# Two pairs of blocks merged, and idle products on TensorE at the end of the sorted experts' layer

## The reference

```python
def _L2_attn_ref(x, Wq, bq, Wk, bk, Wv, bv, Wo, bo):      # 16 heads of 16
    q = einsum('btc,hcd->bhtd', x, Wq) + bq;  k = ... + bk;  v = ... + bv
    probs = softmax(q @ k.T * scale + causal)
    return (probs @ v) @ Wo + bo

def _L2_ffn_ref(x, weight, scale, expert_masks, router_w): # top 1 of 32 experts
    p = softmax(x @ router_w)
    return max(p) * (x @ (ternary(weight) * scale * expert_masks[argmax(p)]).T)

def _L3_attn_ref(x, Wq_a, q_norm_w, Wq_b, Wk_rope, Wkv_a, kv_norm_w, Wkv_b, Wo):
    q = rmsnorm(x @ Wq_a, q_norm_w) @ Wq_b                 # latent of 192
    kv = rmsnorm(x @ Wkv_a, kv_norm_w) @ Wkv_b             # latent of 64
    k_rot = rope(x @ Wk_rope)                              # 64, shared by the heads
    return causal_attention(q, kv, k_rot) @ Wo
```

## Time and profile before

| | |
|---|---|
| median of 3 executions | 1505.15 us (1503.67 to 1508.03) |
| profiled execution, its own time | 1509.29 us |
| its span, first to last instruction | 1506.8 us |
| busy in the span | PE 1308.7, DVE 790.2, ACT 588.9, POOL 416.4 us |
| mean granted TensorE clock | 0.927 of full |

### The profile page before, as it was taken

One profiled execution on the slowest core, in us unless ns is written; L12 is line 12 of the kernel. 1 busy time (PEld: TensorE's weight loads), 2 busy tenths in 40 slices (PEclk: granted clock), 3 DMA queues, 4 the chain that ended last, 5 costly groups with the idle time before them and its releaser, 6 DMA issues. The chain is left out here.

```text
span 1506.8 us, 29274 instructions
## 1 busy us (share of the span) xinstructions
PE 1308.7 (87%) x12212; PEld 1002.6 (67%) x12235; DVE 790.2 (52%) x1491; ACT 588.9 (39%) x1067; POOL 416.4 (28%) x346
## 2 busy tenths in 40 slices
PE   6879989979989979899979889999779578969988
PEld 3468985559957667788747667888755234557555
DVE  5734465553272633433528556888245547943543
ACT  4612224483534653334412521223324333641551
POOL 0063302034730000445320105443011219921100
PEclk9979999989989999999978889999889789989999
DMA  4000003054041001000090060000044210000000
GB/s 107 0 2 4 3 4 113 1 118 96 1 130 60 2 1 32 1 0 1 1 263 31 21 216 1 1 1 2 1 162 154 73 19 1 2 1 29 2 1 28
DMA packets 75266, 63.56 MB, mean 42 GB/s; under 512 B 21240, under 2 KB 73152, under 8 KB 75008
## 3 DMA queue, kind: packets, MB, share of 16 engines
q1 hardware_dynamic: 72320, 58.90, 13.7%
q0 software_dynamic: 768, 2.10, 0.4%
q10 hardware_dynamic: 2048, 0.70, 0.2%
HBM read 53.29 MB, written 8.39 MB: 41 GB/s over the span
## 5 line engine op out<-in xcount | busy, mean ns | idle before, releaser
L1796 PE MATMUL ps<-rounded 128*128 128x512 f32 x384 | 92.9, 398 | 5.9 <-DVE work L1928 5.3
L1482 POOL TENSOR_TENSOR work<-weights,work 32x512 f32<-32x512 f32 x64 | 85.9, 1342 | 17.9 <-DVE work L1469 14.0
L1264 POOL TENSOR_TENSOR fixed<-fixed,cross 128x768 f32<-128x768 f32 x32 | 58.8, 1838 | 110.7 <-DVE cross L1213 110.7
L1796 PEld LDWEIGHTS ps<-rounded 128*128 128x128 f32 x384 | 72.2, 191 | 24.6 <-issue 6.3
L1178 PE MATMUL ps<-rounded 128*128 128x256 f32 x576 | 79.5, 294 | 6.8 <-DVE rounded L1232 4.1
L1827 POOL TENSOR_TENSOR rounded<-weights,rounded 128x256 fp32r<-128x256 f32 x32 | 23.6, 757 | 205.3 <-ACT rounded L1845 205.3
L1178 PEld LDWEIGHTS ps<-rounded 128*128 128x128 f32 x576 | 73.3, 197 | 10.2 <-DVE rounded L1232 4.4
L211 PE MATMUL ps<-fixed 128*128 128x128 f32 x160 | 35.8, 352 | 46.7 <-ACT fixed L199 28.3
L211 PEld LDWEIGHTS ps<-fixed 128*128 128x128 f32 x160 | 20.6, 169 | 60.1 <-issue 33.0
L716 DVE TENSOR_TENSOR fixed<-fixed,ps 128x512 f32<-128x512 f32 x12 | 8.2, 687 | 99.2 <-PE ps L632 99.2
L1928 DVE TENSOR_TENSOR work<-work,ps 128x512 f32<-128x512 f32 x32 | 22.0, 687 | 68.4 <-ACT work L1862 66.3
(11 more groups left out here) (472 smaller groups left out, 3239.8 us busy)
## 6 DMA issues: line engine op xcount, KB each, us to landing
weights<-in_L_ffn_masksT SPq DMA_DIRECT2D x32, 256.0 KB, 6.3
weights<-in_L_ffn_fc_w SPq DMA_DIRECT2D x16, 256.0 KB
weights<-in_L_xattn_Wq SPq DMA_DIRECT2D x2, 2048.0 KB, 9.9
weights<-in_L_xattn_WoT SPq DMA_DIRECT2D x2, 2048.0 KB, 10.2
sorted_in<-work SPq DMA_DIRECT2D x1, 3072.0 KB, 10.6
work<-sorted_in SPq DMA_DIRECT2D x12, 256.0 KB, 3.0
sorted_out<-work SPq DMA_DIRECT2D x12, 256.0 KB, 2.1
weights<-in_L_ffn_Wg SPq DMA_DIRECT2D x8, 256.0 KB, 6.1
```

Source lines behind the costliest of these rows:

```text
L1264: nc.gpsimd.tensor_tensor(ro[:, v % 2, :, :], ro[:, v % 2, :, :], sn, ALU.add).then_inc(s["roped"], 1)
L1482: last = nc.gpsimd.tensor_tensor(qb[64 + 32 * half:96 + 32 * half, 2 * (u % 2) + e, tok], cs[made, v % 2, :], sn[made, v % 2, :], ALU.add)
L1796: last = nc.tensor.matmul(ps[:, 2 * (n % 2) + i, :], a[:, q % 2, i, c, :], b[:, c, half * BANK:(half + 1) * BANK], start=c == 0 and part = ...
```

## The change

It has three parts.

1. **L2_attn**: the two blocks become one. TensorE goes from the keys' products to the values' products, and waits only for the copy of the queries whose banks the values take (`queries`, 1 for the first eight sequences, 2 for the rest). The first scores wait for the copied keys (`keys`) too. POOL clears `vblk` first, then adds the bias to `x`, then clears `blank`. SP's clearing DMA stands behind the same loads as before, now in this block.
2. **L3_attn**: the two blocks ahead of the attention become one. DVE handles the latents in two halves of four tiles, ACT's queue interleaves squares, the two roots and the repeated part, TensorE turns each half behind the latents, and the copies out are shared: ACT takes the first half and one of the two last copies (`values`), DVE the second half and the other. `hold(k, 7, 10)` takes the place of `hold(k, 6, 10)`.
3. **L2_ffn**: `hold(k, 2, 48)` after the last `apply`, and `hold(k, 2, 4)` after the first and after the second `norm_turn`.

```diff
@@ stage_L3_attn, the first two blocks
-    with k.stage("sorted", "lat", "sq", "mean", "std", "rstd", "qn", "km", "kvn", "kra", "krb") as (block, s):
+    lat = qb[0:64, 3, :]
+    with k.stage("sorted", "lat", "sq", "mean", "std", "rstd", "qn", "dup", "kvn", "kra", "krb", "vzero", "t_qn", "t_km", "c_qn", "c_km",
+                 "c_lat", "t_kv", "kvs") as (block, s):
+        def copied(eng, scaled, copy, g):
+            eng.wait_ge(s["t_qn"], g + 1)
+            for a in range(2):
+                ins = scaled(qnT[:, a, g * BANK:(g + 1) * BANK], ps[:, 4 * g + a, :], (w.qw, w.qw_low)[a][:, 1:2])
+            ins.then_inc(s["c_qn"], 1)
+            eng.wait_ge(s["t_km"], g + 1)
+            copy(kk[:, g * BANK:(g + 1) * BANK], ps[:, 4 * g + 2, :]).then_inc(s["c_km"], 1)
+            for jp in range(2):
+                ins = copy(lat[...], ps[0:64, 4 * g + 2, ...])
+            ins.then_inc(s["c_lat"], 1)
+        def values(eng, copy, jj):
+            eng.wait_ge(s["t_kv"], 1)
+            eng.wait_ge(s["vzero"], 1)
+            copy(kvt[rows, :, jj, :], ps[rows, 3, :]...).then_inc(s["kvs"], 1)
@@ TensorE, behind the eight latents
+            for g in range(2):
+                pe.wait_ge(s["krb"], g + 1)
+                pe.wait_ge(s["kvn"], 4 * g + 4)
+                pe.wait_ge(s["dup"], 4 * g + 4)
+                (8 transposes of qn, then_inc t_qn; 4 transposes of km, then_inc t_km)
+            hold(k, 7, 10)
+            pe.wait_ge(s["c_lat"], 2)
+            (8 transposes of lat, then_inc t_kv)
@@ ScalarE
+            for j in range(5):
+                squares(j)
+            root(0)
+            squares(5)
+            again(0)
+            again(1)
+            squares(6)
+            again(2)
+            again(3)
+            squares(7)
+            root(1)
+            copied(act, ..., nc.scalar.copy, 0)
+            for j in range(4, NT):
+                again(j)
+            values(act, nc.scalar.copy, 0)
@@ VectorE: for g in range(2), on tiles 4g to 4g+3
+                dve.wait_ge(s["lat"], 4 * g + 4)
+                dve.wait_ge(s["sq"], 8 * g + 8)
+                (rope products, means, rope sum, reciprocal, scaling, as before on half the tiles)
+            copied(dve, ..., nc.vector.tensor_copy, 1)
+            values(dve, nc.vector.tensor_copy, 1)
@@ stage_L2_ffn, TensorE
                 apply(b)
+            hold(k, 2, 48)
             for i in range(NT // 2):
                 norm_turn(k, s, pe, i, (0, 1))
+                if i < 2:
+                    hold(k, 2, 4)
@@ stage_L2_attn, the two blocks in one
-    with k.stage("bk", "qk", "copied", "xb") as (block, s):
...
-    with k.stage("v", "vzero", "vals", ...) as (block, s):
+    with k.stage("bk", "qk", "queries", "keys", "xb", "v", "vzero", "vals", ...) as (block, s):
             for b in range(BATCH):
+                if b % 8 == 0:
+                    pe.wait_ge(s["queries"], b // 8 + 1)
...
                 if u == 0:
                     pe.wait_ge(s["vals"], 4)
+                    pe.wait_ge(s["keys"], 4)
...
             nc.gpsimd.memset(vblk, 0.0).then_inc(s["vzero"], 1)
+            pool.wait_ge(w.sem, w.loaded)
+            nc.gpsimd.tensor_tensor(x, x, bc(w.bo, 1, NT), ALU.add).then_inc(s["xb"], 1)
             nc.gpsimd.memset(blank, 0.0).then_inc(s["blank"], 1)
...
             normalise(7)
+            dve.wait_ge(s["xb"], 1)
```

More of the change, by code:

```diff
@@ L1350, in _, with squares @@
                         nc.gpsimd.tensor_copy(to[:, :, n, e, :], of[:, :, e, n, :]).then_inc(s["sorted"], 1)
+            nc.gpsimd.memset(kvt, 0.0).then_inc(s["vzero"], 1)
         @block.scalar
         def _(act):
-            for j in range(NT):
+            def squares(j):
                 act.wait_ge(s["lat"], j + 1)
@@ L1360, in _, with root, again @@
                 nc.scalar.activation(sq[:, 0:64], ps[:, j, 192:256], ACT.Square, accum_out=ss[:, 1, j:j + 1]).then_inc(s["sq"], 1)
-            act.wait_ge(s["mean"], 2)
-            nc.scalar.activation(rstd, ss, ACT.Sqrt).then_inc(s["std"], 1)
-            for j in range(NT):
+            def root(g):
+                act.wait_ge(s["mean"], 2 * g + 2)
+                nc.scalar.activation(rstd[:, :, 4 * g:4 * g + 4], ss[:, :, 4 * g:4 * g + 4], ACT.Sqrt).then_inc(s["std"], 1)
+            def again(j):
@@ L1389, in stage_L3_attn @@
[L1389 to L1392, removed]
-            for g in range(2):
[L1394 to L1432, removed]
@@ L2308, in stage_L2_attn, with _ @@
     mx, sm, rs = k.work.take(2, 16), k.work.take(2, 16), k.work.take(2, 16)
-    with k.stage("bk", "qk", "copied", "xb") as (block, s):
+    blank = k.work.take(D)
+    with k.stage("bk", "qk", "queries", "keys", "xb", "v", "vzero", "vals", "scored", "maxed", "centred", "expd", "summed", "recip", "probs", "turned", "copied", "pv",
+                 "yT", "out", "added", "blank", "cleared", *NORM_SEMS) as (block, s):
+        @block.sync
+        def _(sp):
+            sp.wait_ge(s["blank"], 1)
+            sp.dma_start(k.sorted_in.rearrange("(b p) d -> p b d", p=P), bc(blank, 1, TILES)).then_inc(s["cleared"], 16)
+            sp.wait_ge(s["cleared"], 16)
         @block.tensor
@@ L2319, in _ @@
                     last.then_inc(s["qk"], 1)
[L2321 to L2339, removed]
-            for m in range(2):
-                act.wait_ge(s["qk"], m + 3)
-                for g in range(2):
-                    nc.scalar.activation(kexp[:, m, g, :], ps[:, 4 + 2 * m:6 + 2 * m, :].rearrange("p a b -> p (a b)"), ACT.Identity,
-                                         bias=bk[:, g, m:m + 1], scale=w.pmask[:, g:g + 1]).then_inc(s["copied"], 1)
-    blank = k.work.take(D)
-    with k.stage("v", "vzero", "vals", "scored", "maxed", "centred", "expd", "summed", "recip", "probs", "turned", "copied", "pv",
-                 "yT", "out", "added", "blank", "cleared", *NORM_SEMS) as (block, s):
-        @block.sync
-        def _(sp):
-            sp.wait_ge(s["blank"], 1)
-            sp.dma_start(k.sorted_in.rearrange("(b p) d -> p b d", p=P), bc(blank, 1, TILES)).then_inc(s["cleared"], 16)
-            sp.wait_ge(s["cleared"], 16)
-        @block.tensor
-        def _(pe):
             for b in range(BATCH):
+                if b % 8 == 0:
+                    pe.wait_ge(s["queries"], b // 8 + 1)
                 for g in range(2):
@@ L2441, in _ @@
         def _(act):
+            act.wait_ge(w.sem, w.loaded)
+            act.wait_ge(s["bk"], 2)
+            for m in range(2):
+                act.wait_ge(s["qk"], m + 3)
+                for g in range(2):
+                    nc.scalar.activation(kexp[:, m, g, :], ps[:, 4 + 2 * m:6 + 2 * m, :].rearrange("p a b -> p (a b)"), ACT.Identity,
+                                         bias=bk[:, g, m:m + 1], scale=w.pmask[:, g:g + 1]).then_inc(s["keys"], 1)
             for u in range(8):
@@ L2455, in _ @@
         def _(dve):
+            dve.wait_ge(w.sem, w.loaded)
+            for g in range(2):
+                nc.vector.tensor_scalar(bk[:, g, :], w.bias[:, 1, :], w.pmask[:, g:g + 1], None, ALU.mult).then_inc(s["bk"], 1)
+            for m in range(2):
+                dve.wait_ge(s["qk"], m + 1)
+                nc.vector.tensor_scalar(qT[:, m, :], ps[:, 2 * m:2 * m + 2, :].rearrange("p a b -> p (a b)"), w.bias[:, 0, m:m + 1], None,
+                                        ALU.add).then_inc(s["queries"], 1)
             dve.wait_ge(s["vzero"], 1)
```

49 lines of the change are left out of this document (32 added, 17 removed).

## The result

The changed kernel takes 1487.51 us (median of 4, 1485.06 to 1489.28) against 1506.59 us of the kernel before (4 runs, 1503.67 to 1512.43). The ratio is 0.9867, interval [0.9833, 0.9902]: 19 to 20 us less, where 16.3 was forecast. The profiled execution's span is 1487.6 against 1506.8 us.

The account below looks back on a forecast made before the run. No engine is busy throughout: the kernel is a row of stages, each ending with its own wait. Savings of 10.4, 3.4 and 2.9 us make 16.7, less 0.4: 1505.15 becomes 1488.9 us, range 1483 to 1496.

Parts of the forecast that it names:

- What bound L2_attn: L2_attn: TensorE idle from 772.5 to 780.2 because the block change between keys and values waits for SP's queue.
- 10.4 us for L2_attn: L2_attn merged: values start right behind the keys, 8.0 us saved, and run at full clock, 2.4 us.
- rivals 2 and 3: L2_attn score loop: two more units at half clock, 1495.7 us, chance 0.10; or loop stays down, 1508.9 us, chance 0.03.
- Rival 4: L2_attn: something other than the block change holds the values, such as the queue of loads; 1498.9 us, chance 0.05.
- 3.4 us for the idle products: L2_ffn: idle products hidden by the gathers' wait keep the clock up; latents save 3.3 us, the last turn some 0.2.
- rival 1: L2_ffn: the idle products don't carry the clock to the latents; 1491.9 us, chance 0.20.
- 2.9 us for L3_attn: L3_attn merged in halves: 14.9 us instead of 17.8 from last latent to attention block; saving between 1.6 and 4.9.
- The sum: Whole kernel: three parts' savings total 16.7 us, less 0.4, so 1505.15 becomes 1488.9 us; chance 0.62.
- less 0.4: Whole kernel: 0.4 us taken off the sum, since every later clock dip falls on other work than before.

Follow-up runs that it names:

- e5_lateloads: The kernel before, both L2_attn blocks kept, SP issuing the loads of L2_xattn's weights in the second block: 1502.61 against 1508.67 us, ratio 0.9967.
- the first two of the four side by side: On one chip: the changed kernel again, 1487.6 us; and it without the 56 idle products, ACT's last L3_attn repeated parts ahead of its copies, 1488.47 us.
- the new order: The changed kernel with ACT's four last repeated parts of L3_attn ahead of its copies of the first half: 1486.8 us, ratio 0.9863.
- e4_noholds: The kernel before with the L2_attn and L3_attn merges, without the 56 idle products of L2_ffn: 1489.33 us, ratio 0.9875.
- e8_overrun: The changed kernel with 96 idle products instead of 48 behind the last `apply` of L2_ffn: 1492.46 us, ratio 0.9897.

## Why the prediction was right or wrong

**What bound L2_attn: right.** It rested on reading the pause as SP's queue and not as work of the layer. The late loads showed it (6.1 us back without any merge).

**10.4 us for L2_attn: right.** 10.7 in the trace, 10.6 with this part alone. The values took 7.26 us (7.2 forecast) and began with the keys' end. The dips of the clock in the loop stayed in their place, so rivals 2 and 3 fell: 55.45 us for the loop against 55.23, and 54.53 with this part alone. Rival 4 fell with the profile after: the values follow the keys without a pause while the same loads are still being issued.

**3.4 us for the idle products: the term that was mis-sized.** In its place the runs show 0 to 1.5 us: nothing with this part alone ([0.9983, 1.0016]), and 0.9 us between the first two of the four side by side, to which the new order's 0.6 is to be added. Two things were off. In two of the four traces with 48, 4 and 4 of them (the changed kernel's first and that of the idle products alone) the clock was down for a part of the latents, 11.8 and 11.7 us, which is rival 1, given 0.20; in the other two they took 10.07. In all four the clock fell once on the way, in the changed kernel's first profile in the first latents, in the other three among the turns; what differed is when it was back. It stayed at 1.00 up to the last latent only with 70 idle products and with 104. And the price was read from one execution in which the clock was down for longer than usual: latents of 13.06 us, where six other traces without idle products show 11.5 to 11.7. Against those there was 1.5 us to win, not 3.

**2.9 us for L3_attn: mis-sized the other way.** The time shows 5.8 us with this part alone; the traces with the same order show 5.4 to 5.8, and 4.2 and 4.6 where the clock was down for longer there (`e4_noholds`, `e8_overrun`: the ten idle products took 4.05 and 3.63 us instead of 2.71). The steps were right up to the second half's turns, which wait for the repeated parts behind ACT's copies. The sizes were not. I took 0.44 us for a repeated part from eight in 3.52 us, but there each waited for DVE's pair of scalings; four in a row take 1.13 us. With the shorter repeated parts ACT was never behind: the last squares end 0.8 us after they start, not 1.5. The second root comes at 1.8 instead of 2.8, as DVE's part ahead of it was 0.3 us shorter too. ACT's copies of a half took 2.24 us, not 2.65, and so the second half's turns start at 5.3 instead of 7.3. The part behind them, 7.0 us in this trace, was forecast between 5.6 and 8.9, 7.6 in the middle.

**The sum: right, partly by errors that cancel.** 10.4, 3.4 and 2.9 were forecast, less 0.4; the runs with one part each show 12.3, 0.2 and 5.8 us less, of which the traces place 10.6, nothing and 5.8 in the parts. So the two errors, 1.9 to 3.4 us too much for the idle products and 2.9 us too little for L3_attn, nearly cancel, and that the sum comes out within 1.4 us is in part luck. The -1.84, 3.28, 1.13 and -0.94 of the table are work that the change doesn't touch; together they gave 1.6 us here, where I took 0.4 off. That is a draw too: another profile of either kernel gives other values.

## What to carry to other kernels

A block change waits for every queue, a queue that only issues DMAs too: before you price a pause between blocks, look at what ends last, and ask whether it can be issued later or the blocks joined. A duration taken from a row with other work between its instructions is the pace of that work; take the time of an instruction from a stretch in which it runs back to back. And the price of a dip in the clock taken from one profile is one draw: compare several executions before a term rests on it. The same holds for an experiment's trace: a gain counts for an edit only if it lies in the stretch that the edit touches.

## What the runs showed of the hardware

The granted clock fell in the score loop of L2_attn while TensorE's busy time was 6.31 of 7.00 us, in products of 32 rows by 64 columns. The Trainium skill, "TensorE: Matmul & The Clock Gate", section "A second HAM failure mode: psum-queue depth-cycling", describes swings of the clock under small idle times between groups of products; the traces agree that it swings in this loop, and do not show which property of the products is the cause.

The same program placed its dips differently from one execution to the next: the changed kernel's latents took 11.77 us in one profile and 10.07 in another. L2_xattn's attention up to the router took 216.5 to 220.1 us over the nine traces of the first two sets of kernels that leave it as it is (`e5_lateloads` loads its weights later). That is more than two of the three parts were forecast to save. The places are not arbitrary either. The ten traces with the merged L2_attn show two cases only: 54.5 us for the loop and 262.0 for the row with L2_xattn, or 55.4 and 260.1 to 260.3. The changed kernel's own two profiles are one of each. What decides between them is not shown.
